# Queries' halves in two PSUM banks and by channel tile, their copies issued by two engines, and another order in the last batch's attention

## What is computed

```python
def wkv(r, k, v, w, u, time_emb):           # two scans over time, forward and backward
    decay = exp(-exp(w)) * (0.5 + 0.5 * tf)
    num, den = nf + nb - ekv + euk * v, df + db - ek + euk
    return sigmoid(r) * (num / maximum(den, 1e-8)) * (0.8 + 0.2 * tf)

def attn(x, w_qkv, b_qkv, w_out, b_out):    # 16 heads of 16 channels, causal
    q, k, v = heads(x @ w_qkv.T + b_qkv)
    p = softmax(q @ k.T / 4 + causal)
    return merge(p @ v) @ w_out.T + b_out

x = x + attn(wkv(x, side, side, w1, u1, cond), ...)
y = wkv(x, side, side, w2, u2, cond)
x = x + (silu(y @ Wu.T) * (y @ Wg.T)) @ Wd.T   # Wu, Wg, Wd rounded to -1, 0, 1 times a scale
```

## Time and profile before

| | |
|---|---|
| time, median of 3 runs | 175.5 us (175.47 to 176.79) |
| the profiled execution | 175.76 us, of which the span of the core's instructions is 173.9 us |
| busy: TensorE, VectorE | 146.8 us (84%), 147.5 us (85%) |
| busy: ScalarE, GpSimd | 115.5 us (66%), 54.8 us (32%) |
| mean granted TensorE clock | 0.996 of full |
| SyncE's stack copies | 24 of 128 KB |

### The profile page before, as it was taken

The page is one execution under the profiler, slowest core; times in us unless marked ns, Lnnn a source line. Parts: engine busy times, 40 slices in busy tenths (PEclk is TensorE's granted clock), DMA queues, the critical chain, the costliest instruction groups (busy, mean ns, idle before and its releaser), DMA issues.

```text
span 173.9 us, 3854 instructions
## 1 busy us (share of the span) xinstructions
PE 146.8 (84%) x1558; PEld 97.7 (56%) x1558; DVE 147.5 (85%) x255; ACT 115.5 (66%) x184; POOL 54.8 (32%) x57
## 2 busy tenths in 40 slices
PE   0007897977999799999999899999998999998992
PEld 0007882333378457754675567536855675787781
DVE  0599998999999999999958999994689999575673
ACT  2557976989877566598657354985572547886560
POOL 8800052999930086521000655310002232000000
PEclk9999999999999999999999999999999999999998
DMA  4899413505001323645630065347310000010001
GB/s 105 343 432 424 175 62 121 107 19 115 9 2 60 124 55 66 121 80 99 161 135 19 6 121 105 77 80 188 102 61 0 0 8 0 4 64 0 4 2 60
DMA packets 7290, 16.15 MB, mean 93 GB/s; under 512 B 936, under 2 KB 4456, under 8 KB 6888
## 3 DMA queue, kind: packets, MB, share of 16 engines
q1 hardware_dynamic: 5544, 10.52, 16.0%
q0 software_dynamic: 1440, 5.24, 15.3%
q10 hardware_dynamic: 288, 0.14, 0.4%
HBM read 6.43 MB, written 1.05 MB: 43 GB/s over the span
## 4 chain that ended last, share of the span: by engine, by line
PE 36%; DVE 23%; issue 6%; ACT 4%; POOL 2%; POOLq 1%; DVEq 0%; ACTq 0%
DVE row_max L711 7%; PE attn_ps L1144 7%; PE acc_ps L1068 4%; PE attn_ps L1039 3%; PE wide L1222 3%; PE wide L1117 2%; PE attn_ps L1234 2%; DVE hid L779 2%; PE wide L1122 2%; PE acc_ps L1004 2%; PE turn_ps L1004 2%; POOL hid_lo L296 2%; PE attn_ps L1186 2%; DVE x_hi L730 1%; PE turn_ps L1199 1%
## 5 line engine op out<-in xcount | busy, mean ns | idle before, releaser
L267 POOL TENSOR_TENSOR extra<-extra,k_t 128x512 f32<-128x512 f32 x7 | 10.0, 1426 | 62.4 <-DVE x_lo L736 43.4
L711 DVE TENSOR_REDUCE row_max<-wide 128x4 f32<-128x1024 f32 (+1 forms) x24 | 28.7, 1214 | 0.6 <-PE wide L1097 0.6
L428 ACT ACTIVATE probs<-wide 128x1024 f32<-128x1024 f32 x24 | 23.8, 1018 | 2.9 <-PE wide L1122 1.9
L466 ACT ACTIVATE silu<-attn_ps,up_scale 128x256 f32<-128x256 f32 x24 | 11.2, 473 | 21.4 <-PE attn_ps L1039 21.4
L624 DVE TENSOR_TENSOR_SCAN fwd<-decay,ek 128x256 f32<-128x256 f32 x32 | 23.1, 768 | 0.0
L636 DVE TENSOR_TENSOR_SCAN bwd<-ek,decay 128x255 f32<-128x255 f32 x32 | 20.2, 678 | 0.0
L1242 PE MATMUL wide<-ones 128*128 128x128 f32 x24 | 5.3, 421 | 14.0 <-DVE fwd L827 14.0
L296 POOL TENSOR_TENSOR hid_lo<-hid,hid_hi 128x512 f16<-128x512 f32 x9 | 11.1, 1239 | 15.0 <-ACT hid_hi L473 15.0
L1039 PE MATMUL attn_ps<-x_hi,w_tern 128*128 128x256 f16 x96 | 14.3, 274 | 1.1 <-DVE x_hi L730 1.0
L1039 PE MATMUL attn_ps<-x_lo,w_tern 128*128 128x256 f16 x96 | 13.9, 273 | 1.2 <-DVE x_lo L736 1.2
L1144 PE MATMUL attn_ps<-probs,v_pad 128*32 128x256 f32 (+1 forms) x192 | 12.6, 334 | 0.7 <-ACT probs L428 0.6
(11 more groups left out here) (156 smaller groups left out, 339.0 us busy)
## 6 DMA issues: line engine op xcount, KB each, us to landing
stack<-halves SPq DMA_DIRECT2D x24, 128.0 KB, 2.1
fwd<-extra POOLq DMA_DIRECT2D x5, 512.0 KB, 4.8
fwd<-bwd POOLq DMA_DIRECT2D x5, 512.0 KB, 4.4
w_raw<-wup_d SPq DMA_DIRECT2D x1, 1024.0 KB, 11.5
w_raw<-wgate_d SPq DMA_DIRECT2D x1, 1024.0 KB, 13.2
w_raw<-wdown_d SPq DMA_DIRECT2D x1, 1024.0 KB, 14.9
wqkv<-wqkv_d SPq DMA_DIRECT2D x1, 768.0 KB, 7.2
k_t<-k_d SPq DMA_DIRECT2D x1, 768.0 KB, 8.6
```

What stands on the lines that cost most here:

```text
L428: nc.scalar.activation(probs[:, j, :], flat(wide[j % 2][:, :, :]), ACT.Exp, scale=SOFTMAX_SCALE).then_inc(prob_done, 1)
L466: nc.scalar.activation(silu[:, e % 2], up, ACT.Silu, scale=up_scale[:, 0:1]).then_inc(silu_done, 1)
L711: nc.vector.tensor_reduce(out, src, AX.X, ALU.max).then_inc(max_done, 1)
```

## The change

Five things are changed; the rest of the program is as it was.

1. The queries' second channel tile is projected into `wide[0][:, 0, 0:T]` (`q_bank`), the first one stays in `acc_ps`. TensorE waits for the fifth exponential of the batch ahead of this projection.
2. ScalarE and VectorE signal each of the queries' tiles by itself. VectorE's low half of a tile waits for that tile's high half alone.
3. SyncE copies the queries' high and low half tile by tile (four copies of 64 KB, the first high copy and the low one). The second high copy (`second_high`, 128 KB, all of r = 2) is issued by GpSimd for batch 0 and by ScalarE, right behind the high halves, for batches 1 to 3.
4. The waits that counted six copies per batch count eight, on two semaphores (`wait_stacks`).
5. In the last batch ScalarE does `first_reciprocal` before `exp_probs(b, 4)` and `tail_sigmoid` before `exp_probs(b, 5)`. TensorE does `tail_project(0)` before the last score tile, and `tail_project(1)` before one of the half-tile products of half 0 that stood ahead of it.

```diff
+        def wait_stacks(engine, n):
+
+            engine.wait_ge(second_in, 16)
+            engine.wait_ge(stack_in, 16 * (8 * n - 1))
+
+        def second_high(engine, b):
+            engine.wait_ge(zeros_q, 2)
+            engine.wait_ge(hi_done[0], CT * (b + 1))
+            if b >= 2:
+                engine.wait_ge(score_t_done, NT * (b - 1))
+            engine.dma_start(stacks[b % 2][2::4, 0, :, :], halves[:, 0, 0, :, :]).then_inc(stack_in if b else second_in, 16)
+
+        q_bank = (acc_ps[:, 0, :], wide[0][:, 0, 0:T])
...
-                for side in (1, 0):
-                    sp.wait_ge(hi_done[side], b + 1)
-                    for r, parts in enumerate(SPREAD):
-                        if parts[side] == 0:
-                            sp.dma_start(stack[r::4, side, :, :], halves[:, side, 0, :, :]).then_inc(stack_in, 16)
-                    sp.wait_ge(lo_done[side], b + 1)
-                    for r, parts in enumerate(SPREAD):
-                        if parts[side] == 1:
-                            sp.dma_start(stack[r::4, side, :, :], halves[:, side, 1, :, :]).then_inc(stack_in, 16)
+                sp.wait_ge(hi_done[1], b + 1)
...
+                for part, done in enumerate((hi_done[0], lo_done[0])):
+                    for ct in range(CT):
+                        sp.wait_ge(done, CT * b + ct + 1)
+                        sp.dma_start(stack[part::4, 0, ct::CT, :], halves[:, 0, part, ct, :]).then_inc(stack_in, 16)
...
             extra_products(1, 0)
-            pool.wait_ge(hi_done[0], 1)
+            second_high(pool, 0)
             values_of_keys(1)
...
+            def high_queries(b):
+                act.wait_ge(qk_done[0], b + 1)
+                if b:
+                    wait_stacks(act, b)
+                for ct in range(CT):
+                    nc.scalar.activation(halves[:, 0, 0, ct, :], q_bank[ct], ACT.Identity,
+                                         bias=vec[:, V_BQ + ct:V_BQ + ct + 1]).then_inc(hi_done[0], 1)
+                if b:
+                    second_high(act, b)
...
+                    if not more:
+                        first_reciprocal(1, b)
                     exp_probs(b, 4)
                     if more:
-                        high_halves(b + 1, 1)
+                        high_keys(b + 1)
                     else:
-                        first_reciprocal(1, b)
+                        tail_sigmoid()
                     exp_probs(b, 5)
...
+            def low_queries(b):
+                if b:
+                    wait_stacks(dve, b)
+                for ct in range(CT):
+                    dve.wait_ge(hi_done[0], CT * b + ct + 1)
+                    nc.vector.scalar_tensor_tensor(
+                        halves[:, 0, 1, ct, :], q_bank[ct], vec[:, V_BQ + ct:V_BQ + ct + 1],
+                        halves[:, 0, 0, ct, :], ALU.add, ALU.subtract).then_inc(lo_done[0], 1)
...
+                if side == 0 and b:
+                    pe.wait_ge(prob_done, NT * (b - 1) + 5)
...
                     for j in range(2, NT):
+                        if j == NT - 1:
+                            tail_project(0)
                         tail_score_t(j)
                         if j < NT - 1:
                             tail_weigh(j - 2)
-                    tail_project(0)
...
-            for part in range(2):
-                for e in range(2):
-                    tail_up_gate(e, (0,), part)
+            for e in range(2):
+                tail_up_gate(e, (0,), 0)
+            tail_up_gate(0, (0,), 1)
             tail_project(1)
+            tail_up_gate(1, (0,), 1)
             tail_up_gate(2, (0,))
```

69 lines of the change are left out of this document (37 added, 32 removed).

## The result

The changed kernel takes 178.45 us in the median of 4 runs (177.69 to 179.3), the kernel before 175.49 (4 runs, 175.43 to 176.79): 1.015 of the time before, interval 1.011 to 1.019. I had forecast 176.8 us and a range up to 178.0. It is slower by more than I expected, and outside the range. Two runs near 217 us at a mean clock of 0.68, one of the kernel before and one of a kernel further down, are left out of all that follows.

A forecast was written before the change was run, and what follows sets the result against it. The prediction saw one chain of work changing engine from stretch to stretch, with late first scores staying late. Batch 0 (0.6), batch 1 (0.2), batches 2 and 3 (0) and last batch (0.6) gave +1.4 us: 176.8 us, range 175.1 to 178.0.

The forecast's parts named there:

- The price of SyncE's issues: Batch 0 stack copies: half-size copies issue in 0.60 to 0.65 us each, so first scores and maxima come 0.6 us later.
- Cheap issues: Rival: half-size copies issue in 0.35 us; batch 0 gains 0.3, batch 1 costs nothing; +0.3, 175.8 us; chance 0.15.
- Batch 1: Stack copies of batch 1: one more SyncE issue makes TensorE's first score tile later; +0.2 us (0 to 0.3).
- Batches 2 and 3, ScalarE's issue, the two banks: Later copies in batches 2 and 3, ScalarE's new issue before the reciprocals, TensorE's added bank wait: all covered, 0 us each.
- ScalarE's issue gets on the chain: Rival: a slow ScalarE issue delays the reciprocals, +0.55 us at each of two borders; sum +2.5, 178.0 us; chance 0.13.
- GpSimd's copy: Batch 0, second high copy: takes some 2.8 us, landing at 28.0, before SyncE's last copy, so it adds nothing.
- GpSimd's copy is last: Rival: GpSimd's copy lands at 30.0, batch 0 costs 1.15 us; sum +1.9, 177.4 us; chance 0.10.
- GpSimd beside VectorE: Batch 0: GpSimd's product, some 1.0 us later, shares time with VectorE's scans, which are covered up to about a microsecond.
- The tail: Last batch: the sigmoid delays the last exponential, so last weighing and half 1's output product come 0.6 us late (-0.1 to +0.7).
- Tail not late: Rival: the last exponential finds ScalarE free or its lateness is absorbed behind the product; +0.8, 176.3 us; chance 0.10.
- The sum: Whole kernel: 0.6 + 0.2 + 0 + 0.6 = +1.4 us, forecast 176.8 us; chance as forecast 0.47.

## Why the prediction was wrong, point by point

**The price of SyncE's issues: right.** The 16 half-size copies took 602 ns in the median, and the one extra issue made the scores late. Tile stack in the changed kernel (ns min/median/max):

```profile
L264 SPq DMA_DIRECT2D stack<-halves x16: 529/602/1438, 25.2 to 129.3; - x16
...
L202 ACTq DMA_DIRECT2D stack<-halves x3: 537/537/608, 58.9 to 127.0; - x3
```

The maxima came 0.63 us later (30.26 against 29.63 where the stack starts at 23.2); I had +0.6. *Cheap issues* is false.

**Batch 1: right.** The wait that I named is there, and the delay grew by 0.24 us (part of which may be the clock's) against +0.2:

```profile
63.21 0.59 PE L1133 MATMUL wide<-mask_qk,identity_b 128*128 128x512 bf16 x2 [0.23 <-DMA stack<-halves]
```

**Batches 2 and 3, ScalarE's issue, the two banks: right,** 0 each. The delays in the table don't change from batch 1 to batch 3. *ScalarE's issue gets on the chain* is false: its three issues took 537 to 608 ns.

**GpSimd's copy: right.** It was issued some 0.55 us later than I had it (25.49 against 24.94, the start of GpSimd's product where the stack starts at 23.2), and had landed within 2.9 us (I took 2.8), before SyncE's last. *GpSimd's copy is last* is false.

**GpSimd beside VectorE: mis-sized.** I wrote that the product "shares the time with VectorE's scans before 28.8; those have until 29.94 and are covered up to about a microsecond". The product began 1.33 us later and not 1.0 (26.27 against 24.94, both with the stack started at 23.2), and the scans lost 1.4 us, from 2.81 to 4.19. The cover was misread too: between the scans' end and the maxima VectorE did the scale arithmetic, so that only its wait of 0.57 us was free, and not a microsecond. Two of these rows of before:

```profile
28.73 0.13 DVE L939 TENSOR_SCALAR w_scale<-acc_ps 128x3 f32<-128x3 f32 x1
...
29.21 0.15 DVE L948 TENSOR_SCALAR out_scale<-gd_scale 128x1 f32<-128x1 f32 x1
```

With the scores 0.6 us later the cover was just enough: the maxima started at 30.34 where the copies would have allowed 30.26. I had not worked out what the collision would cost, only what it might, and whoever next removes the late copy runs into it, as the run with whole copies did.

**The tail: right mechanism, 0.42 us where I had 0.6.** TensorE waited 0.32 us for the exponential and not 0.6: shifted back by batch 3's 3.1 us (144.86 against 141.75 before), the exponential ended at 156.54 and not 156.65, and the weighings ahead of it ended at 156.27 and not 156.1 (my own terms, 154.42 + 2 x 0.9, make 156.2, so a part of the 0.6 was a slip in the sum). *Tail not late* is false.

**The sum.** 1.4 us was the forecast and 1.4 us is what the edits cost at the floor, 176.8 us. That they agree so closely is in part luck: the stack cost 0.96 where I had 0.8 and the tail 0.43 where I had 0.6, and the two errors cancel. What failed is the step under the whole sum: "So what is late in the first scores stays late in everything behind them." It holds for work that takes as long as before. I read TensorE's 0.80 us of idle time at 28.96 as something that would grow by 0.6 us and end there, and never asked what its growth does to TensorE. It grew to 1.39 us, with another gap of 1.22 us nine us later, and the clock fell to half in most runs: 0.4 to 2.5 us on top in nine of ten, 1.6 in the median of the four runs of the result and 1.4 in that of all ten. A rival with that mechanism is missing from my list. The profile of before had a hint: its three runs were 175.47, 175.5 and 176.79, and I treated the third as scatter. It was the kernel's second level, so this kernel was already at the edge.

Shown: filling the first gap takes 1.3 us off the changed kernel's median of ten and brings seven of ten runs to within 0.3 us of the predicted sum; lengthening the gap in the kernel before costs 1.1 us in the median with nothing delayed, and every one of its runs then has a mean clock of 0.99 or below; filling both gaps (two kernels) leaves 0 of 22 runs at a higher level and 0 of 22 at 0.99 or below, against 29 and 59 of 93 in the kernel before. Not shown: what decides in a single run whether the clock falls. The same program has runs at each level, and in the kernel with 1.48 us of idle time the first gap was without effect in the profiled run. The Trainium skill ("TensorE: Matmul & The Clock Gate", "What's actually happening") reports that the count of slow products at one kernel's start differs between runs; that the levels here differ from run to run agrees.

## What to carry to other kernels

An issue of a DMA costs its engine the same whether the copy is whole or half, so where an engine is bound by issuing, splitting makes it later; take an issue off it and leave the copies whole. A delay ahead of TensorE has two prices, the time itself and what the longer idle time does to its clock: look at the granted clock and at the gaps around the place, and where the runs of a kernel show two levels, ask which gap makes the second before adding to one. Before taking a wait away, look what stands behind it on each engine: here a weight sum, filling products and a GpSimd product each took its place.

## What the runs showed of the hardware

**Short gaps can halve TensorE's clock for microseconds, in some runs.** In the changed kernel the longest gap was 1.39 us and the engine otherwise busy for most of the time from 29 to 47 us; the low stretches lasted about 3.4 us (30 to 33.4) and about 6.9 us (40.1 to 47). What a low stretch costs depends on its place. From 30 to 33.4 us, where VectorE waits for the scores, it cost 1.04 us. From 37.4 to 40.7, where VectorE had work, it cost at most 0.2 to 0.3 us (175.63 and 175.66 in the two profiles that have it, on a floor of 175.4). The kernel before's second level, 1.2 us above its floor at a mean clock of 0.98, would by the arithmetic above have twice that stretch; none of its runs at that level was profiled.

**A GpSimd instruction holds up VectorE's.** One scan takes 0.66 us alone. The first one in batch 0, before and then in the changed kernel (each alone, ns):

```profile
L624 DVE TENSOR_TENSOR_SCAN fwd<-decay,ek x1: 1071/1071/1071, 26.0 to 26.0; 128x256 f32<-128x256 f32 x1
```

```profile
L655 DVE TENSOR_TENSOR_SCAN fwd<-decay,ek x1: 2445/2445/2445, 25.7 to 25.7; 128x256 f32<-128x256 f32 x1
```

Before, it ended at 27.06, 0.55 us after GpSimd's product (25.24 to 26.51); after, at 28.11, again 0.55 us after the product's end (27.56). In the second case the scan began at 25.67, ahead of the product (26.27) and during GpSimd's DMA issue (25.49 to 26.25), so the issue too seems to have held it; no run separates the two, and which of them holds it stays open. The Trainium skill ("SBUF — State Buffer", "SBUF: two separate sides") says that VectorE, with two inputs from SBUF, and GpSimd take a shared pair of ports by an exclusive lock for a whole instruction, and that the later one waits. The 0.86 us for a 128x1 product beside GpSimd's, which had started 0.7 us before it, agrees. By that rule a scan that started first would not wait for the product behind it, so the product alone doesn't explain the 2445 ns; the page tells of VectorE keeping GpSimd from issuing DMAs, and here it went the other way.
